# Weighted sums of values: one packed word of tile numbers per batch, and half of the one-hots made by ScalarE

## The reference, cut to what matters

```
sums[dst, h*64:(h+1)*64] = sum over edges e into dst of  w[e, h] * v[src[e], h*64:(h+1)*64]
sums[dst, 256 + h]       = sum over edges e into dst of  w[e, h]
sums[dst, 260]           = number of edges into dst
```

## Time and profile before

| what | value |
|---|---|
| median of 3 timed runs | 5336.79 us |
| lowest and highest of them | 5333.91 and 5350.64 us |
| profiled execution: span from first to last instruction | 5709.5 us |
| mean granted TensorE clock in the profiled execution | 0.855 |
| the stage of the change, `attend_phase`, in the profile | from about 900 to 1267 us of the span |

### The profile page before, as it was taken

The page is one execution under the profiler, slowest core; times in us unless marked ns, Lnnn a source line. Parts: engine busy times, 40 slices in busy tenths (PEclk is TensorE's granted clock), DMA queues, the critical chain, the costliest instruction groups (busy, mean ns, idle before and its releaser), DMA issues. The chain is left out here.

```text
span 5709.5 us, 67954 instructions
## 1 busy us (share of the span) xinstructions
PE 4142.4 (73%) x19769; PEld 3142.0 (55%) x19769; DVE 2438.6 (43%) x4746; ACT 1163.7 (20%) x2671; POOL 2168.6 (38%) x2090
## 2 busy tenths in 40 slices
PE   5788884654816666799976999455559999555668
PEld 2555553443614444599975888333437677334445
DVE  4577778877234444356655000421223222212244
ACT  1233330001220000232322444100004333000023
POOL 0566654554436666000000210466650000566621
PEclk9888887996958888899986999677779999777789
DMA  2677874530743223210012998233330000233310
GB/s 77 208 243 241 250 215 151 162 98 23 235 128 88 85 86 86 86 38 8 7 41 82 336 323 281 89 88 93 87 97 26 1 1 16 75 91 88 91 37 23
DMA packets 375879, 639.34 MB, mean 112 GB/s; under 512 B 73053, under 2 KB 270072, under 8 KB 375424
## 3 DMA queue, kind: packets, MB, share of 16 engines
q1 hardware_dynamic: 275262, 342.97, 18.4%
q0 software_dynamic: 100288, 292.14, 17.6%
HBM read 526.37 MB, written 108.57 MB: 111 GB/s over the span
## 5 line engine op out<-in xcount | busy, mean ns | idle before, releaser
L2554 PE MATMUL sum_ps<-gathered_rows,hit 128*125 (+1 forms) x3328 | 1061.5, 477 | 842.0 <-issue 561.2
L2468 POOL DMA_INDIRECT gathered_rows<-k_table,index x1176 | 1160.8, 987 | 1281.1 <-ACT index L2457 717.6
L2554 PEld LDWEIGHTS sum_ps<-gathered_rows,hit 128*125 128x125 f32 (+1 forms) x3328 | 744.9, 235 | 1158.0 <-issue 1033.1
L97 POOL DMA_INDIRECT rows_all<-kv_table,src_of_visit x416 | 448.5, 1078 | 310.6 <-issue 135.5
L2538 DVE TENSOR_TENSOR node_sums<-node_sums,sum_ps 125x256 f32 x244 | 102.3, 419 | 918.0 <-DMA composed<-in_L_gnn_b 495.7
L2457 ACT ACTIVATE index<-src_of_chunk 128x4 int32<-128x4 int32 x294 | 59.2, 205 | 1647.0 <-DMA gathered_rows<-k_table,index 1581.1
L777 PE MATMUL ps_q<-q,hit_t 125*128 x832 | 322.5, 473 | 5.9 <-issue 5.2
L1057 PE MATMUL ps_sum<-summand,hit 128*125 128x261 f32 x832 | 211.6, 397 | 147.1 <-DVE odd_sums L1017 123.2
L2538 DVE TENSOR_TENSOR window_sums<-window_sums,sum_ps 126x256 f32 x344 | 144.8, 421 | 348.2 <-PE sum_ps L2554 183.0
L2762 PE MATMUL qk_ps<-window_sums,composed 128*128 128x126 f32 (+1 forms) x2400 | 292.1, 279 | 0.0
L1996 DVE TENSOR_TENSOR y<-out_ps,b 128x256 f32<-128x256 f32 x120 | 50.9, 424 | 551.2 <-PE out_ps L1895 464.0
(11 more groups left out here) (478 smaller groups left out, 6714.6 us busy)
## 6 DMA issues: line engine op xcount, KB each, us to landing
w<-in_L_ffn_W SPq DMA_DIRECT2D x112, 1024.0 KB
v_kept<-rows_all SPq DMA_DIRECT2D x104, 512.0 KB
v_rows<-v_kept SPq DMA_DIRECT2D x104, 512.0 KB, 3.6
gathered_rows<-k_table,index POOLq DMA_INDIRECT x1176
w<-in_L_ffn_w SPq DMA_DIRECT2D x64, 256.0 KB
b<-in_L_ffn_b SPq DMA_DIRECT2D x88, 128.0 KB
y_slots<-y SPq DMA_DIRECT2D x32, 256.0 KB
y_slots<-y SPq DMA_DIRECT2D x56, 128.0 KB
```

Of the source, the lines that this page charges most:

```text
L97: pool.indirect_dma_start(env.ring[:, k % KEPT_RING, i, :], None, env.kv_table, bass.IndirectOffsetOnAxis(env.src_of_visit[:, k * VB + i:k ...
L2468: pool.indirect_dma_start(self.rows[:, (q % SLOTS) * CHUNKS + c, :], None, self.table, bass.IndirectOffsetOnAxis(self.index[:, q % SLOTS, ...
L2554: mm = pe.matmul(sum_ps[0:rows, k % banks, 0:D], hit[:, g % (lead + 1), i * chunks + c, :], gather.rows[:, ds(first[i] + c, 1), :].rearran ...
```

## The change

Per batch, VectorE no longer loads four tile numbers but one word, in which the four numbers stand at five bits each, and takes them out with shifts and masks in registers. The words (`tiles_of_batch`, one per batch) are made once in `setup_phase` by five more VectorE instructions in pass j = 0. The load of a batch's word stands ahead of the wait for `multiplied` of that batch.

The one-hots of a batch are split by visit. VectorE makes those of visits 2 and 3 by comparison as before, 256 columns instead of 512. ScalarE makes those of visits 0 and 1: `Abs` of the difference between column number and `rel_dst` into a buffer `distance` with two slots, 128 columns at a time, and then `Relu` of 1 minus that for both visits at once. The differences of batch k+1 are measured ahead of ScalarE's wait for the slot of batch k. TensorE gets one more wait, for ScalarE's half.

```diff
+                    else:
+                        of_batch = tile_bc[j][0:1, 0:VT].rearrange("p (k i) -> p i k", i=VB)
+                        done(v.tensor_copy(word[:], of_batch[:, VB - 1, :]))
+                        for i in reversed(range(VB - 1)):
+                            done(v.scalar_tensor_tensor(out=word[:], in0=word[:], scalar=float(WORD), in1=of_batch[:, i, :],
+                                                        op0=ALU.mult, op1=ALU.add))
+                        done(v.tensor_copy(env.tiles_of_batch[:], word[:]))
...
-                def tile_of(k, i):
-                    return v.value_load(env.tile_of_visit[0:1, k * VB + i:k * VB + i + 1], min_val=0, max_val=T - 1)
+                def tiles_of(k):
+                    word = v.value_load(env.tiles_of_batch[0:1, k:k + 1], min_val=0, max_val=WORD ** VB - 1)
+                    return [((word >> (5 * i)) & (WORD - 1)).with_bounds(min_val=0, max_val=T - 1) for i in range(VB)]
...
                         v.tensor_tensor(here, here, ps_sum[0:P, k % 2, i, 0:VC], ALU.add).then_inc(summed, 1)
-                        if k + 1 < batches:
-                            following.append(tile_of(k + 1, i))
-                    return following
 
                 def hits(k):
-                    make_hits(v, env, hit[:, k % SLOTS], env.rel_dst, 128, k).then_inc(hits_made, 1)
+                    v.tensor_tensor(hit[:, k % SLOTS, ACT_HITS:VB, :],
+                                    env.iota[:, 0:128].unsqueeze(1).to_broadcast([128, VB - ACT_HITS, 128]),
+                                    env.rel_dst[:, k * VB + ACT_HITS:(k + 1) * VB].unsqueeze(2).to_broadcast([128, VB - ACT_HITS, 128]),
+                                    ALU.is_equal).then_inc(hits_made, 1)
...
-                tiles = [tile_of(0, i) for i in range(VB)]
                 for k in range(batches):
+                    tiles = tiles_of(k)
                     v.wait_ge(multiplied, k + 1)
                     if k + SLOTS < batches:
                         hits(k + SLOTS)
-                    tiles = add(k, tiles)
+                    add(k, tiles)
...
             @block.scalar
             def _(act):
+                def measure(k):
+                    if k >= 2:
+                        act.wait_ge(act_hits, k - 1)
+                    for i in range(ACT_HITS):
+                        ins = act.activation(distance[:, k % 2, i, :], env.iota[:, 0:128], ACT.Abs,
+                                             bias=env.rel_dst[:, k * VB + i:k * VB + i + 1], scale=-1.0)
+                    ins.then_inc(measured, 1)
+
                 act.wait_ge(cleared, 3)
+                measure(0)
                 for k in range(batches):
+                    if k + 1 < batches:
+                        measure(k + 1)
                     if k >= SLOTS:
                         act.wait_ge(multiplied, k - SLOTS + 1)
+                    act.wait_ge(measured, k + 1)
+                    act.activation(hit[:, k % SLOTS, 0:ACT_HITS, :], distance[:, k % 2], ACT.Relu, bias=env.ones[:, 0:1],
+                                   scale=-1.0).then_inc(act_hits, 1)
...
                     pe.wait_ge(copied, k + 1)
+                    pe.wait_ge(act_hits, k + 1)
```

More of the change, by code:

```diff
@@ L68 @@
 SLOTS = 4
+WORD = 32
 def batch_loop(engine, total, head, block):
@@ L196, in setup_phase @@
         ring_row = sb(env, st, "ring_row", [QUADS, 2])
+        word = sb(env, st, "word", [1, VT // VB])
         passes = [(4, P, T, VT_PAD, None), (1, P, T, env.quads.visits, env.quads), (2, WN, NW, env.pairs.visits, env.pairs)]
@@ L955 @@
 VC = D + HEADS + 1
+ACT_HITS = VB // 2
 def attend_phase(env):
@@ L969, in attend_phase @@
         summand = sb(env, st, "summand", [128, SLOTS, VB, VC])
+        distance = sb(env, st, "distance", [128, 2, ACT_HITS, 128])
         odd_sums = sb(env, st, "odd_sums", [P, T, VC])
@@ L973, in attend_phase @@
         cleared, hits_made, multiplied, summed, weighed, copied = [ph.sem() for _ in range(6)]
-        own_landed = ph.sem()
+        own_landed, measured, act_hits = [ph.sem() for _ in range(3)]
         landed = [ph.sem() for _ in range(deep)]
@@ L1006, in _ @@
             def _(v):
-                def tile_of(k, i):
-                    return v.value_load(env.tile_of_visit[0:1, k * VB + i:k * VB + i + 1], min_val=0, max_val=T - 1)
+                def tiles_of(k):
+                    word = v.value_load(env.tiles_of_batch[0:1, k:k + 1], min_val=0, max_val=WORD ** VB - 1)
+                    return [((word >> (5 * i)) & (WORD - 1)).with_bounds(min_val=0, max_val=T - 1) for i in range(VB)]
                 def add(k, tiles):
-                    following = []
                     for i in range(VB):
@@ L3339, in build @@
         env.tile_of_visit = sb(env, x_stack, "tile_of_visit", [1, VT_PAD], I32)
+        env.tiles_of_batch = sb(env, x_stack, "tiles_of_batch", [1, VT // VB], I32)
         env.src_of_visit = sb(env, x_stack, "src_of_visit", [128, VT_PAD], I32)
```

## The result

| kernel | median us | lowest to highest | runs |
|---|---|---|---|
| before | 5336.42 | 5333.91 to 5350.64 | 4 |
| after | 5290.91 | 5281.05 to 5291.53 | 4 |

The ratio is 0.9908, with a 95% interval of 0.9891 to 0.9926. The medians differ by 45.5 us (the interval is 40 to 58); 31.9 were forecast. The profiled execution of after took 5290.56 us, of which the span is 5288.4. Its weighted-sum stage, from the first one-hot to the last addition, takes 308 us where before took 346.

What follows compares the result with a forecast made beforehand. VectorE, its `hit` blocked by GpSimd at shared ports, paces the weighted-sum stage. Gains of 29.0 (100 batches), 1.3 (first `hit`s) and 2.8 (last batches), less 1.2 setup, make 31.9 us off 5336.79: 5305 us, range 5235 to 5340.

Steps and rivals of the forecast that it cites:

- port loop: Weighted-sum stage: VectorE's `hit` stands still until GpSimd's multiplication ends; two batches from 6.42 to 5.84 us; chance 0.52.
- the `hit`'s tail behind GpSimd: Weighted-sum stage: VectorE's comparison ends 0.29 us after GpSimd's weighing in place of 0.55, a loss of 0.26.
- Halving the mean: Rejected reading of the `hit`'s 1.27 us as work: 0.64 would go, loop 5.46, time about 5285.
- The split at no cost: VectorE's queue: shifts and masks hide under other work, and fourth addition to next `hit` stays 0.65 us.
- split costs more: Rival, VectorE's queue ahead of the `hit`: splitting costs more than the loads saved, slower, 5386 or 5416 us; chance 0.11.
- gain is eaten: Rival: s between 0.9 and 1.3, or additions stay 1.75 apart; no change, 5321 to 5345 us; chance 0.13.
- s: Exposed us per batch of splitting the word on VectorE's queue; between 0 and 1.2, taken at the low end.
- Setup and the last batches: Five setup instructions add 1.2 us (0.8 to 1.7); three late batches without `hit` go from 3.04 to about 2.1 each.
- short cycle: Rival, weighted-sum stage: `hit` reaches the ports before GpSimd, 2.06 us a batch; 5219 us if held throughout; chance 0.21.
- in part: Short cycle held for only some batches of the weighted-sum stage; chance 0.21 for part or throughout together.
- Its condition: Short cycle: VectorE back at its next `hit` within 1.77 us of the last one's end; needs 1.57, leaving 0.20.
- a third of the batches: Case of the short cycle held for a third of the weighted-sum stage's batches: about 5275 us.

Runs made afterwards that it cites:

- run 9: The changed kernel with each batch's word loaded twice, the first result unused; 5308.88 us, ratio 0.9934 against before.
- run 3: ScalarE's half alone: ScalarE makes the one-hots of visits 0 and 1, four value loads stay as before; 5328.41 us, ratio 0.9971 against before.
- run 10: The changed kernel, unchanged, profiled a second time; 5292.59 us.
- run 11: The kernel before, unchanged, for a third profile; 5332.9 us.
- runs 2 to 9: Eight variants: parts of the change alone, or the changed kernel with other waits, transfer places, one-hot split or loads; 5202.8 to 5328.41 us.
- run 2: The word alone: packed word kept in the changed kernel, VectorE makes all four one-hots, ScalarE none; 5295.64 us, ratio 0.9925 against before.
- run 4: The changed kernel with GpSimd weighing batch k only once VectorE's one-hot of k is made; 5254.27 us, ratio 0.9844 against before.
- runs 7 and 8: The changed kernel with ScalarE making all one-hots, 5236.52 us; the same with own rows' loads behind every sixteenth batch, 5202.8 us.
- run 5: The changed kernel with the nodes' own rows loaded behind every sixteenth batch, not every fourth; 5298.98 us, ratio 0.9921 against before.

## Why the prediction was right or wrong

The direction was right, the time lies in the range, and the gain was larger than forecast, 45.5 us against 31.9.

*The port loop.* Right, term by term. Forecast 5.84 for two batches, measured 5.87: the `hit`'s tail behind GpSimd 0.29 (0.29), the additions 1.46 (1.43). The `hit` between 905 and 1105 has a mean of 1290 ns, where the earlier trace rows had 1271 with twice the columns. Halving the mean would have been wrong, as said: that time is waiting.

*The split at no cost.* Right. At most two operations of 0.045 us and one of 0.057 for the address stand before an addition, under the addition before it; 0.66 from the fourth addition to the next `hit` (839.60 to 840.26), as in the earlier trace rows. The rivals "split costs more" and "gain is eaten" had their condition in s above 0.9, and s is about 0.

*Setup and the last batches.* +1.60 (forecast +1.2, bound 1.7). The batches without a `hit` are 1.96 apart in place of the 3.04 of the earlier trace rows; forecast 2.1. (Their first additions start at 1107.85, 1109.81, 1111.77 and 1113.73.)

*ScalarE.* Right: `Abs` 394 ns, `Relu` 507, copy 202, together 1.50 a batch (forecast 1.45, though its terms add up to 1.43), never waited for, no table load.

*The step that failed: that the port loop holds throughout.* It was given 0.52 and the short cycle 0.21. What happened is the mixture that the rival described, "in part": some 30 batches at 2.05 (forecast 2.06). Its condition held about as worked out: VectorE has 0.20 to spare. In after a `hit` that came 2.12 behind the last was still ahead of GpSimd (825.66); those 2.31 and 2.25 behind the last were not (840.26, 907.01). 0.5 more on the queue (run 9) never let it hold; four loads (run 3) neither. And since issues come late at fixed places, the short cycle came back only where GpSimd had waited for rows. The price of the mixture was mis-sized: a third of the batches was put at 5275, and it came to 5291. The term left out is GpSimd's waits for rows. I had written that transfers would grow to 189 GB/s, which is the port loop's demand in bytes. The short cycle's I didn't work out, nor the 10 us or so that the rows behind a part of the own rows come late.

Runs 9 and 10 give the sizes, as estimates. With the port loop alone the stage takes 317.1; without its wait for rows (4.2) and the 2.9 of the last batches that is 310. After has 308.1 and 306.9, without the waits for rows (27.5 and 27.0) about 280. So the short cycle gives back some 30 us (30 batches by 0.88 would be 26) and the waits take 23 of it away again. The timed gains point the same way, 27 us and 45.5, though their single runs overlap; of these 18 us the profiles have 9 to 10 in this stage.

That the time came out so near the forecast is in part luck: in this stage the gain that the forecast left out and the waits that it left out nearly cancel.

*What stays open.* The stage gains 38 us (346 to 308), the setup loses 1.6; that leaves 9 of the 45.5 elsewhere. In the profiles as much and more lies in the stage that computes the scores, ahead of this one, whose code is the same in both kernels. TensorE's starts there, before again and after (ns min/median/max, first to last start):

```profile
L777 PE MATMUL ps_q<-q,hit_t x832: 377/382/793, 182.8 to 760.2; 125*128 x167
```

```profile
L786 PE MATMUL ps_q<-q,hit_t x832: 377/382/794, 181.7 to 742.9; 125*128 x167
```

577 us against 561, and 569 (run 11) against 559 (run 10). But runs 2 to 9, with the same code there, lie anywhere between 559 (run 2) and 576 (run 3). The setup's 1.6 don't show at its start either, which is no later in after. What sets this stage's length wasn't tried; it is no effect of the one-hots or loads that a run here shows.

## What to carry to other kernels

When a stalled instruction and the one that stalls it take turns, ask which of them arrives first: shortening what comes before the victim can turn the order round and give more than its own length, and a slack of 0.2 us then decides (2.05 or 2.93 us a batch here). A gain that hangs on such slack is better written into the kernel as an order (run 4), or the instruction that stands still is moved to another engine (runs 7 and 8; with the transfers spread, three times the gain). And work out, for each speed that a stage could reach, how long its transfers take beside it, one by one and not by their bytes alone.

## What the runs showed of the hardware

Two stable rhythms of the same instructions were not expected to alternate within one stage. A comparison of 256 columns took 0.43 us when it came ahead of GpSimd's multiplication and 2.02 us when it came just behind its start (840.26); GpSimd's took 1.90 when it was first and 2.08 when it came behind the comparison's start. The Trainium skill (SBUF — State Buffer, section "SBUF: two separate sides") says that whichever of the two starts first gets the port pair for the whole instruction; the trace agrees in both directions.

A wait elsewhere can mend an order. With the 27.5 us of GpSimd's waits for rows gone (run 5) the stage was only 8 shorter, since each wait had let VectorE come back in front.

A transfer of 625 KB in packets of 1 KB held back the rows behind it by 9.1 to 13.3 us, while 512 KB in packets of 4 KB landed 1.25 us behind the 512 KB before.

A value load of one word from SBUF is 0.303 us on VectorE's queue with 0.190 and 0.023 behind it, and a shift or mask is 0.045; so one load with seven such operations, 0.83 together, is cheaper than two loads.
